# ScalarE keeps the last columns of a half as it takes the PSUM bank over; GpSimd makes eight C products of sixteen

## The reference

```
xz = LN(x) @ in_proj_w.T ; xc, z = split(xz)             # 512 + 512 channels
u  = causal conv over 4 taps of xc, + conv_b
dt = clip(sigmoid(u @ dt_w.T + dt_b), 1e-4, 1)
for each token t, channel d, state n (16 states):
    s[d,n] = exp(clip(dt[d] * A[d,n], -5, 5)) * s[d,n] + dt[d]*B[n]*u[d] + 1e-6
    y[d]   = sum over n of s[d,n] * C[n]  + D[d]*u[d]
x = x + (y * silu(z)) @ out_w.T
x = x + top-2-of-8 experts and one shared expert of LN(x)
```

## Time and profile before

| | us |
|---|---|
| median of 3 runs | 2950.19 |
| lowest, highest | 2948.59, 2950.59 |
| profiled execution, its own time | 2948.53 |
| its span | 2946.7 |
| busy in the span: PE | 2601.8 (88%) |
| PEld | 2291.2 (78%) |
| DVE | 2246.7 (76%) |
| ACT | 2030.5 (69%) |
| POOL | 2235.6 (76%) |

### The profile page before, as it was taken

The page is one execution under the profiler, slowest core; times in us unless marked ns, Lnnn a source line. Parts: engine busy times, 40 slices in busy tenths (PEclk is TensorE's granted clock), DMA queues, the critical chain, the costliest instruction groups (busy, mean ns, idle before and its releaser), DMA issues.

```text
span 2946.7 us, 49244 instructions
## 1 busy us (share of the span) xinstructions
PE 2601.8 (88%) x15616; PEld 2291.2 (78%) x15616; DVE 2246.7 (76%) x4890; ACT 2030.5 (69%) x4675; POOL 2235.6 (76%) x1354
## 2 busy tenths in 40 slices
PE   7888888888888888888888888888887599999998
PEld 4777877878787778877877778787776488888887
DVE  2989999999998999899989989998998233333332
ACT  3878888888888888888888888888875133333332
POOL 2989998989898989889998989898986033333333
PEclk9889999999999989999999999899987699999999
DMA  4222222222222222222222222222221288888886
GB/s 171 83 77 76 77 77 83 77 76 86 92 83 80 78 84 85 77 88 79 77 76 82 79 76 82 94 85 80 73 81 35 95 199 202 201 202 201 202 200 152
DMA packets 138184, 309.67 MB, mean 105 GB/s; under 512 B 15040, under 2 KB 79680, under 8 KB 137792
## 3 DMA queue, kind: packets, MB, share of 16 engines
q1 hardware_dynamic: 110848, 270.03, 29.5%
q0 software_dynamic: 27072, 36.46, 6.2%
HBM read 258.42 MB, written 48.01 MB: 104 GB/s over the span
## 4 chain that ended last, share of the span: by engine, by line
PE 52%; DVE 22%; ACT 10%; issue 8%; POOL 2%; DMA 1%; SPq 0%; DVEq 0%; ACTq 0%; POOLq 0%
PE bank L662 13%; DVE bank L1242 10%; PE bank L680 9%; PE bank L563 7%; PE bank L600 6%; DVE room L1242 4%; PE bank L552 4%; DVE room L1251 4%; ACT bank L809 3%; ACT room L793 3%; PE bank L530 2%; PE bank L580 2%; PE bank L616 2%; PE bank L570 2%; PE bank L644 2%
## 5 line engine op out<-in xcount | busy, mean ns | idle before, releaser
L1031 POOL TENSOR_TENSOR room<-dtu,b_all 128x1024 f32<-128x1024 f32 x512 | 1202.6, 2370 | 26.4 <-DVE dtu L1419 13.5
L809 ACT ACTIVATE bank<-room,eps_col 128x512 f32<-128x512 f32 x1024 | 693.9, 683 | 282.6 <-DVE carry L1256 202.4
L793 ACT ACTIVATE room<-room,neg_a 128x256 f32<-128x256 f32 x2048 | 867.9, 497 | 0.8 <-DVE room L1208 0.8
L600 PE MATMUL bank<-ident,room 128*128 128x128 f32 x4096 | 589.8, 295 | 236.8 <-DVE room L1251 215.7
L600 PEld LDWEIGHTS bank<-ident,room 128*128 128x128 f32 x4096 | 513.1, 153 | 302.1 <-DVE room L1251 232.3
L1020 POOL TENSOR_TENSOR room<-room,c_all 128x1024 f32<-128x1024 f32 x224 | 532.1, 2375 | 122.9 <-DVE bank L1242 87.7
L1242 DVE TENSOR_TENSOR_SCAN bank<-room,carry,bank 128x256 f32<-128x256 f32 x864 | 580.5, 735 | 48.6 <-ACT bank L809 47.7
L1156 POOL DMA_INDIRECT out<-room,ids x144 | 223.8, 1554 | 409.8 <-DMA out<-room,ids 217.9
L1321 DVE SCALAR_TENSOR_TENSOR hid<-hid,bank 128x256 f32<-128x256 f32 (+1 forms) x312 | 131.1, 420 | 453.8 <-ACT hid L904 453.7
L1242 DVE TENSOR_TENSOR_SCAN room<-room,carry,bank 128x256 f32<-128x256 f32 x672 | 446.1, 728 | 1.1 <-DVE hot L1292 0.5
L552 PE MATMUL bank<-xnT,w_conv 128*128 128x256 f32 x3072 | 404.2, 288 | 7.0 <-ACT xnT L832 5.5
(11 more groups left out here) (150 smaller groups left out, 3095.4 us busy)
## 6 DMA issues: line engine op xcount, KB each, us to landing
b_all<-b_scratch SPq DMA_DIRECT2D x128, 512.0 KB, 4.0
c_all<-b_scratch SPq DMA_DIRECT2D x128, 512.0 KB, 5.5
room<-in_wgu SPq DMA_DIRECT2D x72, 704.0 KB, 5.9
room<-in_wd SPq DMA_DIRECT2D x72, 384.0 KB, 3.6
room<-x_by_expert SPq DMA_DIRECT2D x72, 260.0 KB, 2.9
x_in<-in_x SPq DMA_DIRECT2D x32, 256.0 KB, 6.1
x<-in_x SPq DMA_DIRECT2D x32, 256.0 KB, 2.7
out<-x SPq DMA_DIRECT2D x32, 256.0 KB, 4.2
```

What stands on the lines that cost most here:

```text
L600: last = mm(tr_bank[k][:, b * P:(b + 1) * P], v[n % VRING][:, b, k * P:(k + 1) * P], ident[:, :], is_transpose=True, start=False, stop=(n ...
L793: last = af(da[n % RING][:, b, :], dt[c.par][:, b, :], ACT.Exp, scale=neg_a[:, b, n:n + 1])
L809: af(v_slot(c, n, h)[:, :], v[n % VRING][:, 2 * h:2 * h + 2, :].rearrange("p b t -> p (b t)"), ACT.Identity, bias=eps_col[:, 0:1]).then_in ...
L1031: nc.gpsimd.tensor_tensor(out=v[n % VRING][:, :, :], in0=dtu[:, :, :], in1=row, op=ALU.mult) \
```

## The change

GpSimd takes state 14's C product as well, so that it makes the eight even ones and VectorE the eight odd ones. VectorE's copies of the last columns go. ScalarE makes them instead: in `bank_free`, where it has just waited for VectorE's product of the half whose bank it is about to overwrite, it copies the two columns to `carry`, waits for that copy, and goes on to its eps copy. At position 3 it waits only for the product, as before. VectorE's scans of the next chunk wait for the new semaphore `half_kept` in place of `dve_kept`, with the same counts.

```diff
-BY_POOL = [0, 2, 4, 6, 8, 10, 12]
+BY_POOL = [0, 2, 4, 6, 8, 10, 12, 14]
@@ scalar
+            def keep_half(c, n, h):
+                last = v_slot(c, n, h)[:, :].rearrange("p (j t) -> p j t", j=2)[:, :, TC - 1]
+                af(carry[:, n, 2 * h:2 * h + 2], last, ACT.Copy).then_inc(half_kept, 1)
+                act.wait_ge(half_kept, kept(c, n)[1] + h + 1)
+
             def bank_free(c, n, h):
                 if n in BY_POOL:
                     act.wait_ge(half_ready, halves(c, n) + h + 1)
-                elif c.pos != 3:
-                    act.wait_ge(dve_kept, kept(c, n)[1] + h + 1)
                 else:
                     act.wait_ge(dve_product, products(c, n)[1] + h + 1)
+                    if c.pos != 3:
+                        keep_half(c, n, h)
@@ vector, scans
-                    dve.wait_ge(dve_kept, by_dve)
+                    dve.wait_ge(half_kept, by_dve)
@@ vector, c_times_state
-                    last = v_slot(c, n, h)[:, :].rearrange("p (j t) -> p j t", j=2)[:, :, TC - 1]
-                    if c.pos != 3:
-                        vec_e.tensor_copy(carry[:, n, 2 * h:2 * h + 2], last).then_inc(dve_kept, 1)
```

More of the change, by code:

```diff
@@ L255, in build @@
         dve_product = sem("dve_product")
-        dve_kept = sem("dve_kept")
+        half_kept = sem("half_kept")
         norm_step = sem("norm_step")
```

## The result

The changed kernel took 2,996.99 us (median of 4 runs, 2,994.67 to 2,997.46) against 2,949.4 before: the ratio is 1.016, with a 95% interval of 1.0147 to 1.0173. It is slower by 47.6 us, where 25 were forecast (2,975, range to 2,992): the direction holds, the size is nearly twice the forecast one and 5 us past the end of the range.

The account below looks back on a forecast made before the run. Bound: a ring through GpSimd's queue, product 4 to product 4. Three turns of 70.14, one of 68.45 and 0.7 for the seam make 279.6 against 276.2; +3.4 over 7.5 groups is +25 us: 2,975, range 2,952 to 2,992.

Parts of the forecast that it names:

- a ring through GpSimd, not VectorE: GpSimd's product 4 to the next body's product 4: 67.42 us before, 70.14 after at positions 0 to 2.
- The rival that all 65 us come off: VectorE bounds the kernel, so its 65 us of removed work come off: 2,885 us, chance 0.13.
- GpSimd +2.34: State 14's C product in GpSimd's slot 15 delays everything queued behind it by 2.34 us per body.
- product 10 late by 0.38: Two ScalarE copies between tanh and state 10's column copy delay GpSimd's product 10 by 0.38 us at positions 0 to 2.
- the 0.06 that the prediction takes off: Time by which a bank came free after its VectorE product, subtracted from two ScalarE copies' 0.44 us.
- product 4 to product 8 is a chain of 18.00 us: From GpSimd's product 4 through ScalarE's u, TensorE's projections, tanh and column copy to product 8: 18.00 us.
- 23.7 from product 4 to product 10 at position 3: GpSimd's stretch at position 3, 24.52 us before, shortens to 23.7 as about 0.8 of ScalarE's lead goes.
- The seam: Second path, through TensorE's restart between two bodies: 70.8 us at position 2, 0.7 over the ring, under it elsewhere.
- the third rival: Slower still: the restart's eight extra transposes cost 1.8 us at every position, +5.2 per four bodies, 2,989 us, chance 0.24.
- the 0.9 that was taken for position 2: Eight more TensorE transposes at the restart between bodies, priced at full clock: 0.9 us.
- ScalarE's copies behind the second tanh: State 9's two copies add 0.38 us to the ring; state 11's push only the z gate, priced at nothing.
- VectorE's saving priced at nothing: VectorE's 65 us of removed products and copies turn into waits at y's gating, the residual add and scans.

Follow-up runs that it names:

- e7: Changed kernel plus both short fills of useless TensorE matmuls, four ahead of the B/C projection and eight at the seam between bodies: 2,970.4 us.
- e1: Changed kernel with ScalarE still copying the last columns but GpSimd making only seven C products, without state 14's: 2,992.1 us.
- e5: Changed kernel plus four useless matmuls in TensorE's wait ahead of the B/C projection: 2,976.1 us.
- e6: Changed kernel plus eight zero-weight matmuls in TensorE's wait for state 14 at the seam between bodies: 3,014.5 us.
- e12: Kernel before with ScalarE keeping the columns, seven GpSimd products, and fills at the seam and ahead of the B/C projection: 2,952.2 us.
- e9: Kernel before plus matmuls that add 0 in TensorE's seam waits, three for state 14 and four for state 15: 2,968.1 us.

## Why the prediction was right or wrong

- *The bound (a ring through GpSimd, not VectorE):* right for this change. Turn for turn the ring with the clock held is what was worked out (e7), and the kernel gets slower while VectorE is relieved of 60 us of busy time. The rival that all 65 us come off is out. The ring is not the only path, though: e1 leaves it at 67.9 us and is 44 us slower.
- *GpSimd +2.34, product 10 late by 0.38:* right (2.30 and 0.38 to 0.40). A little luck is in the second: ScalarE's copy costs 0.19 and not 0.22, and two of them are 0.38 without the 0.06 that the prediction takes off.
- *The step that failed:* "So product 4 to product 8 is a chain of 18.00 us", carried over unchanged, and with it 23.7 from product 4 to product 10 at position 3. It holds TensorE's work at full clock. In the kernel after u comes later relative to TensorE, whose wait ahead of the B/C projection grows from 1.42 to 2.12 us at position 2 and from 0.29 to 2.13 at position 3, and the clock falls behind it: 19.63 from product 4 to product 8 at position 2 and, at position 3, 25.31 from product 4 to product 10 (1148.74 to 1174.05). That is +1.6 for each of two bodies in four, 3.2 x 7.5 = 24 us; the short fill ahead of the projection (e5) gave back 21 of the 22 that were missing and set product 4 to product 8 at 18.1 us again, and product 4 to product 10 at position 3 at 23.9. I had looked at the clock at the seam alone, where a row showed 0.50, and not asked what a longer wait does where the clock was still full.
- *The seam:* the third rival came nearest in time (2,989), but put the price in the wrong place. A restart at full clock (e6) gained nothing by itself; it moved the half clock to the B/C projection. The forecast had the seam end the turn at position 2, by 0.7. It ended the one into position 1 instead: product 2 waits 0.86 us there, 0.65 in e5, and not at all in e7, which differs from e5 by the fill at the seam alone. From the restart to the residual add are 20.4, 21.0, 19.6 and 19.6 us at positions 0 to 3 (19.1, 19.0, 20.1 and 19.1 before), so that the price of the eight transposes was nowhere the 0.9 that was taken for position 2. How the third rival comes to its +5.2 us is not worked out in the prediction.
- *ScalarE's copies behind the second tanh:* priced at 0.38 in the ring and nothing at the z gate. Right in the presence of the eighth product with the clock held (+10 measured), and badly incomplete as a price of that half: alone it is 26.6 us with the clock held and 44 without.
- *VectorE's saving priced at nothing:* right; the time went to the gating of y (1.07 us), the z gate and the scans, and not to the residual add. The prediction read the idle times in rows 1 a little narrowly: GpSimd's are 4.2 to 7.8 us in a body and not 5 to 7, VectorE's 7.6 at position 0 and not under 6. Nothing in its sum hangs on that.

Open: how ScalarE's copies come to cost e12 3.9 us per four bodies; and the 17 us between ScalarE's copies' price without fills (44) and with them (27) which are put down to the clock's stretches by the sum alone. Which stretch makes how much wasn't tried.

## What to carry to other kernels

Where no engine is full, find the ring (from an instruction to itself in the next turn, through every queue it crosses) and add the change to that; busy shares chose the wrong engine here. One ring is not proof against a second path, so a change in two parts wants each part run alone. Then list every wait of TensorE that the change makes longer and ask what the work behind it costs at half clock if that work is on the ring. Two parts of a change that lengthen parallel paths don't add; price each alone, take the longer, and add only what the other puts on that same path (10 us here).

## What the runs showed of the hardware that was not expected

Work without use can pay. Four matmuls (1.89 us in e5) ahead of one projection bring 21 us in the changed kernel, and with those at the seam 24 us in the kernel before, whose mean granted clock goes from 0.92 to 0.97. The same kind of fill at the seam alone makes both kernels slower (+17.5, +19), and in both traces TensorE comes to the next wait sooner and its clock falls there. The Trainium skill, "TensorE: Matmul & The Clock Gate", section "Why this matters for your kernels", advises against idle gaps between bursts of matmuls; the runs agree, with the addition that filling one gap can open another. The length of the wait alone doesn't decide: behind waits for u of up to 1.91 us the traces that were read show a full clock and behind those of 2.12 to 2.30 (and of 3.3 in e6) a fall, but in e9 a wait of 2.69 us at position 1 was followed by a full clock (1.00 from 1001.00 to 1005.50) and one of the same length at position 2 by a fall. A float32 matmul of 128x512 stands as two instructions of 0.43 us each in the trace (32 in 13.90 us), which a fill has to count.
